# Sixty-five matrix products nobody reads, and a new order of the first bodies

## The reference, cut to what matters

```python
h = layernorm(x) * (1 + ca) + sa
x = x + ga * attention(h)          # 16 heads, |i - j| <= 32, softmax
h = layernorm(x) * (1 + cb) + sb
x = x + gb * ffn(h)                # softmax router, top 2 of 8, plus a shared expert
...
h = silu(xe @ w1[e]) * (xe @ w3[e])
out_routed = out_routed + where(m, h @ w2[e], 0.0)
```

## Time and profile before

| | us |
|---|---|
| median of 3 runs | 704.89 (704.54 to 705.29) |
| profiled execution | 707.2 |
| its span, first to last instruction | 705.5 |
| TensorE busy | 648.6 (92%) |
| VectorE busy | 597.1 (85%) |
| GpSimd busy | 564.8 (80%) |
| ScalarE busy | 555.5 (79%) |

### The profile page before, as it was taken

The page is one execution under the profiler, slowest core; times in us unless marked ns, Lnnn a source line. Parts: engine busy times, 40 slices in busy tenths (PEclk is TensorE's granted clock), DMA queues, the critical chain, the costliest instruction groups (busy, mean ns, idle before and its releaser), DMA issues. The chain is left out here.

```text
span 705.5 us, 19126 instructions
## 1 busy us (share of the span) xinstructions
PE 648.6 (92%) x5940; PEld 552.5 (78%) x5940; DVE 597.1 (85%) x1568; ACT 555.5 (79%) x2458; POOL 564.8 (80%) x667
## 2 busy tenths in 40 slices
PE   3267887999999999999999999999999999999897
PEld 2156676888878888888888888888888888887686
DVE  6545657999989998999999989999998999898685
ACT  3267667998888897989888888989889898986352
POOL 5340344999898998999898989899998899898674
PEclk9999999999999999999999999999999999999999
DMA  5677457968698869697778678796867877743231
GB/s 173 179 144 171 133 135 190 236 172 226 131 271 205 202 160 252 156 244 197 199 194 214 202 219 202 187 225 179 214 191 201 219 190 213 168 120 98 75 127 31
DMA packets 193861, 127.78 MB, mean 181 GB/s; under 512 B 110640, under 2 KB 170720, under 8 KB 193632
## 3 DMA queue, kind: packets, MB, share of 16 engines
q1 hardware_dynamic: 193760, 126.56, 68.8%
HBM read 96.36 MB, written 30.17 MB: 179 GB/s over the span
## 5 line engine op out<-in xcount | busy, mean ns | idle before, releaser
L1174 ACT ACTIVATE p<-ps_s,nmx 128x96 f32<-128x96 f32 x1024 | 331.6, 343 | 38.4 <-DVE nmx L1719 35.3
L1174 ACT ACTIVATION_READ_ACCUMULATOR p<-ps_s,nmx 128x1 f32 x1024 | 213.9, 209 | 0.0
L2661 PEld LDWEIGHTS ps_s<-k,q 128*128 128x128 f32 x1024 | 149.8, 211 | 44.5 <-ACT p L1174 17.1
L2661 PE MATMUL ps_s<-k,q 128*128 128x96 f32 x1024 | 158.3, 293 | 27.0 <-DMA k<-k_scr 13.5
L726 POOL TENSOR_TENSOR xs<-h,sbc 128x512 f32<-128x512 f32 x128 | 165.5, 1300 | 18.1 <-DMA sbc<-s_scr 16.6
L1719 DVE TENSOR_REDUCE nmx<-ps_s 128x4 f32<-128x384 f32 x256 | 137.7, 551 | 46.0 <-PE ps_s L2661 45.6
L732 POOL TENSOR_TENSOR xl<-xs,xh 128x512 fp32r<-128x512 f32 x120 | 153.3, 1283 | 20.2 <-ACT xh L1196 20.1
L2729 PE MATMUL ps_Y<-w2s,g 128*128 128x128 f32 x1152 | 153.5, 279 | 0.4 <-DVE g L1825 0.4
L2729 PEld LDWEIGHTS ps_Y<-w2s,g 128*128 128x128 f32 x1152 | 140.5, 192 | 5.6 <-DVE g L1825 0.7
L1736 DVE STREAM_TRANSPOSE pt<-p 128x384 f32<-128x384 f32 x256 | 133.7, 553 | 1.8 <-PE ps_O L2684 1.1
L1196 ACT ACTIVATE xh<-xs 128x512 fp32r<-128x512 f32 x128 | 79.8, 635 | 35.9 <-POOL xs L726 35.5
(11 more groups left out here) (134 smaller groups left out, 959.1 us busy)
## 6 DMA issues: line engine op xcount, KB each, us to landing
sbc<-s_scr SPq DMA_DIRECT2D x64, 512.0 KB, 6.3
k<-k_scr SPq DMA_DIRECT2D x64, 384.0 KB
q<-q_scr SPq DMA_DIRECT2D x128, 96.0 KB
k<-k_scr SPq DMA_DIRECT2D x32, 336.0 KB
q_scr<-qh SPq DMA_DIRECT2D x32, 256.0 KB, 3.3
k_scr<-kh SPq DMA_DIRECT2D x32, 256.0 KB, 2.7
xr<-x SPq DMA_DIRECT2D x16, 256.0 KB, 3.2
q_scr<-ql SPq DMA_DIRECT2D x16, 256.0 KB, 4.0
```

What stands on the lines that cost most here:

```text
L1174: last = nc.scalar.activation(p[:, n % PRING, gg, :], ps_s[:, n % 2, MK * gg:MK * gg + MK], ACT.Exp, bias=nmx[:, n, gg:gg + 1], accum_out= ...
L2661: last = mm(ps_s[:, n % 2, MK * gg:MK * gg + MK], heads[:, h, gg, nl], k4[:, h, gg, :, MB * nl:MB * nl + MB], start=gg == 0, stop=gg == HG ...
```

## The change

Three things. First, 65 products are added on TensorE whose result nobody reads: 14 on the identity matrix at the start, and 51 of 384 columns by `warm(count)`, one to four in a place, in `fill()` and just ahead of it, down to the last scores of body 1. They write the bank ps_A, which the first expert is the first to use. Second, the first batch's last lines ahead of `fill()` move into it on every engine, with waits added where an order had made them needless, and the order of `fill()` changes in bodies 0 to 4. Third, `body` and `drain` stay as they are.

```diff
@@ TensorE
+            def warm(count):
+
+                for i in range(count):
+                    mm(ps["A"][:, 0:3 * D], wqh[:, 0, :], wqh[:].rearrange("p k d -> p (k d)"), start=True, stop=True)
+
+            pe.wait_ge(cst, IDENT)
+            for i in range(14):
+                mm(ps["A"][:, 0:128], ident[:], ident[:], start=True, stop=True)
             pe.wait_ge(w_in, 112)
+            pe.wait_ge(s_wh, 1)
             pe.wait_ge(s_sl, 1)
...
+            warm(3)
             pe.wait_ge(s_md, 1)
-            pe.wait_ge(cst, IDENT)
             flip(0, l1, ln1, "M1")
             pe.wait_ge(s_wl, 1)
+            warm(4)
             project_q(0)
             project_k(0)
-            project_v(0)
 
             def fill():
 
+                warm(4)
+                project_v(0)
                 scores(0, 0)
                 scores(0, 1)
+                warm(4)
                 scores(0, 2)
+                warm(1)
                 scores(0, 3)
+                flip(1, l1, ln1, "M1")
+                warm(1)
                 scores(0, 4)
-                flip(1, l1, ln1, "M1")
+                warm(3)
                 scores(0, 5)
                 project_q(1)
+                project_k(1)
                 scores(0, 6)
-                project_k(1)
+                warm(3)
+                scores(0, 7)
+                scores(0, 8)
...
@@ SyncE
-            load_bias(0)
-            sp.wait_ge(z_in[0], 1)
-            load_q(0, 0, 0)
-            load_k(0, 0, 0)
-            load_ga(0)
-            load_gb(0)
-            load_bias(1)
...
+                load_q(0, 0, 0)
+                load_k(0, 0, 0)
+                load_bias(0)
+                load_ga(0)
+                load_q(0, 1, 0)
+                load_k(0, 1, 0)
+                load_gb(0)
+                load_bias(1)
@@ GpSimd
+            ones_q(1)
             spread_var(0, l1, ln1)
...
-            add_bias(0)
-            pool.wait_ge(xb_d, 1)
-            ones_q(1)
-            expand_v(0, 0)
-            expand_v(0, 1)
-            gate_wo(0)
...
                 spread_var(1, l1, ln1)
+                expand_v(0, 0)
+                expand_v(0, 1)
+                add_bias(0)
                 inverse(1, l1, ln1)
+                gate_wo(0)
@@ ScalarE
                 probabilities(0, 2, 0)
+                high_h1(1)
                 probabilities(0, 3, 0)
-                high_h1(1)
                 probabilities(0, 4, 0)
+                high_q(1)
                 probabilities(0, 5, 0)
-                high_q(1)
                 high_k(1)
@@ VectorE
                 moments(1, l1, ln1)
+                split_w13()
+                turn_v(0)
+                clear_q()
```

More of the change, by code:

```diff
@@ L800, in fill @@
                 normal(2, l1, ln1)
+                add_bias(2)
                 expand_v(1, 0)
-                add_bias(2)
+                expand_v(1, 1)
                 gate_wo(1)
@@ L1270, in fill @@
                 probabilities(1, 15, 1)
+                expert(0, 0, 0)
                 copy_sums(1)
@@ L2788, in fill @@
                 values(0, 8)
+                warm(1)
+                scores(1, 0)
+                scores(1, 1)
+                turn_sums(0)
+                project_v(1)
                 values(0, 9)
@@ L2792, in fill @@
                 values(0, 12)
-                scores(1, 0)
-                scores(1, 1)
-                turn_sums(0)
-                project_v(1)
-                scores(1, 2)
-                scores(1, 3)
-                scores(1, 4)
-                flip(2, l1, ln1, "M1")
                 values(0, 13)
@@ L2803, in fill @@
                 values(0, 15)
+                warm(1)
+                scores(1, 2)
+                warm(1)
+                scores(1, 3)
+                warm(2)
+                scores(1, 4)
+                flip(2, l1, ln1, "M1")
                 scores(1, 5)
+                warm(3)
+                project_q(2)
                 scores(1, 6)
-                project_q(2)
+                attn_out(0)
+                values(1, 0)
                 scores(1, 7)
-                attn_out(0)
+                warm(1)
                 project_k(2)
-                values(1, 0)
+                scores(1, 8)
+                warm(4)
+                scores(1, 9)
                 values(1, 1)
                 values(1, 2)
-                scores(1, 8)
-                scores(1, 9)
-                scores(1, 10)
-                flip(0, l2, ln2, "M0")
-                scores(1, 11)
-                router(0, 0)
                 values(1, 3)
@@ L2821, in fill @@
                 values(1, 5)
+                flip(0, l2, ln2, "M0")
+                scores(1, 10)
+                scores(1, 11)
+                router(0, 0)
+                warm(1)
+                scores(1, 12)
+                warm(1)
+                scores(1, 13)
+                warm(4)
+                scores(1, 14)
                 values(1, 6)
                 values(1, 7)
-                scores(1, 12)
-                scores(1, 13)
-                scores(1, 14)
-                project_v(2)
+                values(1, 8)
                 router_t(0)
                 scores(1, 15)
+                expert(0, 0)
                 scores(2, 0)
-                values(1, 8)
+                scores(2, 1)
                 turn_sums(1)
-                scores(2, 1)
+                project_v(2)
                 scores(2, 2)
@@ L2851, in fill @@
                 attn_out(1)
+                expert(0, 2)
+                values(2, 0)
                 down(0, 0, 0)
-                expert(0, 2)
                 project_k(3)
-                values(2, 0)
-                values(2, 1)
                 scores(2, 8)
                 scores(2, 9)
+                values(2, 1)
                 down(0, 1, 1)
@@ L2893, in fill @@
                 scores(3, 3)
+                down(0, 6, 0)
+                expert(0, 8)
                 values(2, 12)
@@ L2904, in fill @@
                 expert(1, 0)
+                down(0, 8, 0)
                 project_q(4)
-                down(0, 8, 0)
-                expert(1, 1)
                 scores(3, 6)
                 scores(3, 7)
+                values(3, 0)
+                values(3, 1)
+                expert(1, 1)
                 attn_out(2)
@@ L2952, in fill @@
                 down(1, 6, 1)
+                values(3, 10)
                 values(3, 11)
@@ L2973, in fill @@
                 expert(2, 2)
+                values(4, 0)
+                values(4, 1)
                 project_k(5)
@@ L2997, in fill @@
                 router_t(3)
+                values(4, 8)
                 scores(4, 15)
                 down(2, 4, 0)
+                expert(2, 6)
                 values(4, 9)
```

229 lines of the change are left out of this document (118 added, 111 removed).

## The result

The change made the kernel faster, by less than a third of what I forecast: 701.0 us (median of 20 runs, 696.43 to 707.6) against 704.71 us (20 runs, 703.12 to 708.8), a ratio of 0.9939 with an interval of 0.9918 to 0.996. The 707.6 us was a slow execution and isn't in the ratio. The ratio is an estimate of its own, not the quotient of the medians (0.9947): by the ratio the change won 4.3 us, by the medians 3.7, where I had 13.7. The profiled execution took 700.88 us, 6.3 less than the profiled one of before.

A forecast was written before the change was run, and what follows sets the result against it. TensorE's work was taken to bound the kernel from 160 to 600 us, its low clock to slow the earlier stage. Terms 0.7 + 2.2 + 2.3 + 6.7 + 4.8 = 16.7 us, cut to 14, gave 691 us; range 684.5 to 702.

The forecast's parts named there:

- before 60 us: Sign in body 0: spacing of 512-column products on TensorE falls from 0.43 to 0.23 us before 60 us.
- at the latest before 75: Latest time for 512-column products to come 0.23 us apart; still 0.43 at 100 us would mean the forecast is wrong.
- rival (c): Clock rises only in body 1, or falls again between: 694 to 702 us, 696 at mid-body; chance 0.24.
- ones_q(1), 3.59 us, now lies in GpSimd's wait: At the start, GpSimd's moved copy fits its 4.31 us wait before 11.78; costed at nothing, 0.5 us at worst.
- -0.7 for SyncE's order: At the start, brow's load no longer stands before q's on SyncE: 0.7 us won, first scores near 36.8.
- So before runs at half clock up to the first expert's products: Kernel before: TensorE at 1.2 GHz until about 119 us, read from 512-column products 0.43 us apart, then 0.23.
- it lies 2.3 us above the median of the runs: Profiled execution of before, 707.2 us against median 704.89; forecast 693.2 for the profiled execution became 691 for the median.
- if the clock is high from scores(0,7): Condition of the 16.7 us sum: TensorE at the high clock from scores(0,7), at 52.46 us in body 0, onward.
- the discount: Taken off the 16.7 us sum for a late or falling clock: the 2.2 and 0.5 more, leaving 14 us.
- 2.2 + 2.3, 6.7 and 4.8: Gains in us: body 0's second half (2.2 scores, 2.3 its end), body 1 (6.7), body 2's start (4.8).
- The reordering in bodies 2 to 4 moves work among engines that are then full and removes none: 0, +-1: Bodies 2 to 4: the new order of work is worth nothing, within 1 us either way.
- time won ahead of that reaches the end whole, as long as the other engines keep up: TensorE, busy 435.15 of 440 us between 160 and 600, bounds the kernel there, so earlier gains last to the end.

The follow-up runs named there:

- e2: Kernel before with only GpSimd's copy ones_q(1) moved ahead of spread_var(0): 710.01 us against 706.26, ratio 1.005.
- e1: Changed kernel with only GpSimd's copy ones_q(1) put back behind expand_v(0, 1), ahead of add_bias(0): 698.64 us, ratio 0.9885 to the kernel before.
- e5: e1 without any of the 65 products, so the new order with the copy late: 697.81 us, ratio 0.9871 to the kernel before.
- e3: Changed kernel without any of the 65 products, copy still early: 701.67 us, ratio 0.9948 to the kernel before.
- e4: Changed kernel without the 25 products ahead of the first scores, the 40 others kept: 700.31 us, ratio 0.9909 to the kernel before.
- e9: e7 without any product: 696.59 us, ratio 0.987 to the kernel before.
- e7: e1 with SyncE's put_sums(3) and get_sums(3) moved ahead of load_q(4, 1) in body 4: 694.51 us, ratio 0.9801 to the kernel before.
- e10: e7 repeated unchanged: 697.44 us, ratio 0.9859 to the kernel before.
- e11: e7 without the 25 products ahead of the first scores: 693.4 us, ratio 0.9831 to the kernel before.
- e8: e7 with 79 instead of 51 products of 384 columns, denser in bodies 0 to 2: 697.42 us, ratio 0.987 to the kernel before.
- g3: e8 without the 25 products ahead of the first scores, so 68 late ones: 693.11 us, ratio 0.9788 to the kernel before.
- e12: e8 with 40 more products around the wait for k, meant to have the clock high at the first scores: 694.12 us, ratio 0.9837 to the kernel before.
- g2: e9 repeated unchanged: 697.7 us, ratio 0.9859 to the kernel before.

## Why the prediction was wrong

The direction, and the places at which time is won, came out as predicted: the first expert starts at 98.79 ("near 100"), body 1 takes 32.8 us where I had 31, with ScalarE busy 25.15 of them (77%, "over 75%"), though VectorE with 25.37 is as full. The recorded clock rises inside body 0 (52.2; I had "before 60 us"), but the sign that I had named, 512-column products 0.23 us apart "at the latest before 75", didn't come: they still stand 0.42 us apart at 79.94, and 0.24 first at 84.57. What happened is rival (c), "the clock rises only in body 1, or falls again between", in its second half, and 701.0 us lies at that rival's slow end. It is inside my range too, close to its edge of 702, but that is no merit of the sum, of which these steps failed.

**"ones_q(1), 3.59 us, now lies in GpSimd's wait" of 4.31 us, costed at nothing.** It does lie there, and GpSimd loses nothing. VectorE does: 3.44 us for an instruction of 0.17, csl 3.26 us late, the first scores at 38.37 where I had 36.8, and 0.5% of the time in e2 (1.005) and between the changed kernel and e1 (0.9939, 0.9885). The term that I did have for the start, -0.7 for SyncE's order, was too small: e5, with the copy late and no product, is 1.95 us ahead at the first scores. The copy took that and more. I had looked up whose wait covers the copy, and not who works beside it. The Trainium skill, "SBUF — State Buffer", section "Who interferes with whom", says just this: a VectorE instruction with two inputs in SBUF contends with a GpSimd instruction that reads SBUF, the shared access is an exclusive lock, and the order of issue decides who blocks. The trace agrees: the copy, which reads ident, starts at 7.53, cth with its two inputs at 7.72, and cth ends as the copy does. It agrees the other way round too, in the changed kernel: at 26.75 VectorE starts the two-input w13l (2.56 us), at 26.76 GpSimd its 4-element l_ve, and that takes 2.60 us instead of 0.20.

**"So before runs at half clock up to the first expert's products".** True of the execution that was profiled; of most others it is not, by their mean clock. The clock's gain was sized against a kernel without any, and most executions of before have some of it already. How much this takes off the median can't be given closely: the three runs without an early rise average 708.0 us, the other eighteen about 705.7, so some 2 us. That distance (in the other three sets 0.8, 3.0 and 1.4 us) is about the 2 us between the 6.3 of the two profiled executions and the 4.3 of the ratio. In the prediction it hides in "it lies 2.3 us above the median of the runs": I took that distance over as if it were the same for the changed kernel, whose profiled execution lies on its median.

**The sum's "if the clock is high from scores(0,7)", less 2.7 us.** In the sum this is the largest miss, 2.8 us of 13.3 behind the discount; only the copy cost more time, and the better start hid most of that. The clock was high in 6.8 us of body 0's 29.7 and in 17.8 of body 1's 32.8, and fell each time behind a stretch in which TensorE had idled. The stages' terms, 2.2 + 2.3, 6.7 and 4.8, measured 2.1, 4.8 and 3.6: 10.5 us instead of 16.0 before my discount, and instead of 13.3 behind it. Nor do they belong to the clock alone: e3 gets 0.9948 from the order with no products, and e4 0.9909 without the early ones. I had given the order 0.7 us and a part of the 2.3; with the copy late it alone is worth 1.3% (e5), and it comes with stretches of high clock itself, as all the profiles of kernels without products show (50.6 to 54.1, 74.5 to 77.9 and 84.8 to 88.2 us in e3).

**"The reordering in bodies 2 to 4 moves work among engines that are then full and removes none: 0, +-1" and "time won ahead of that reaches the end whole, as long as the other engines keep up".** The second half held from body 5 on: 6.36 us at max(5,0) are 6.13 at max(15,8). Ahead of that, of the 9.6 us at scores(2,5) on TensorE 1.1 are gone at the maximum of the same block, and 2.1 more between max(4,0) and max(5,0). In the new order TensorE waits for results that hang on rt, the sums' way through DRAM behind q's loads in SyncE's queue: 1.42 us for g at 115.46 in body 2, and 1.66 for o at 194.13 in body 4, where before it waited 0.8 us for g at 200.29. With the sums first the wait in body 4 is gone in every profile; the one in body 2 stays. In time that edit gave between nothing (e5 to e9) and 0.8% (e1 to e7).

So the 14 us of the sum become the 6.4 of the profiles: 1.6 less at the start, 2.8 less in the stages up to scores(2,5), 1.1 in body 2 behind it, 2.1 in body 4. The first two and the last are seen in rows, and two of them (the copy, the wait for rt in body 4) were tested by an edit; why the clock fell, and the wait in body 2, are readings. One small term was off without harm: the 14 products on the identity take 6.32 us instead of 3.8, still inside the wait for csl.

What stays open. What the 25 early products do: e1 and e4 against the changed kernel say nothing; e10 against e11 on one chip (0.9859, 0.9831, intervals overlapping) and e8 against g3 on two (0.987, 0.9788, intervals apart) lean to harm; e7, the same kernel as e10, with 0.9801 leans the other way. They bring the first maximum 1.6 us earlier in the profiles of e7 and e11 (34.55, 36.13), which the end doesn't show. And leads drift in the steady bodies without a wait that I could name: e5's profile is 9.55 us ahead at max(5,0) and 8.57 at max(15,0), e11's 13.42 and 15.03.

## What to carry to other kernels

When work moves into an engine's idle time, ask who runs beside it there, not only what that engine had to do: a GpSimd copy of 3.6 us stopped a VectorE instruction with two inputs in SBUF for as long. Time won early must be followed through every queue behind it, at each place where the same pattern stands: here a small load behind the bulk loads of q cost time in body 4, where it was moved, and in body 2, where it was not. Read the granted clock of several executions before you price a rise of it. Fillers sized to a gap at the low clock fill half of it at the high one; denser ones made the high stretches longer in the profiles, but only without the early products did they also make the kernel faster (g3). A single profile here is good to some 2 or 3 us.

## Unexpected of the hardware

- A GpSimd copy from f32 to fp32r of 4096 elements on 32 partitions (3.60 us) held a 16-element VectorE instruction with two inputs for 3.44 us; alone it takes 0.17. A VectorE instruction with two inputs of 2304 elements (2.56 us), started 0.01 us earlier, held a 4-element GpSimd one for 2.60 us; alone it takes 0.20.
- TensorE's clock falls from 2.4 back to 1.2 GHz in the middle of dense work, after stretches in which it idled (1.96 us busy of 3.40), and full busy time didn't bring it back at once: 12.10 us busy of 12.10 at 0.50 in e12. The Trainium skill, "TensorE: Matmul & The Clock Gate", Part 1, has sustained busy time raise the clock and idle time lower it; the second agrees with the trace, the first only if busy isn't what the profile counts as busy.
- Executions of one and the same kernel on one chip differ in their mean granted clock (0.935 to 1.0), and by some 6 us in time (702.75 to 709.16). The profiles of e9 and g2, the same kernel on two chips, have the first rise at 21.4 and at 47.6 us.
- SyncE's issue of four loads of q took 8.21 us ahead of the sums' transfers in the changed kernel, and 3.24 us behind them in e7; in body 2 the same four took 3.24 us (e8) to 7.07 us (e7) in one and the same order.
